# A perceiver layer: full-size fp32 scores, the 257th key on POOL, values of two batches together, both score pairs of a batch in a row

## The reference, cut to what matters

```python
# q: layernorm(x), 128 x 32 x 128;  k = v = ctx, 128 x 257 x 128;  16 heads of 8 channels
q = queries.reshape(B, L, H, 8); k = keys.reshape(B, 257, H, 8); v = k
scores = einsum('blhe,bshe->bhls', q, k)
A = softmax(scores / sqrt(8), axis=-1) * mask        # mask: 32 x 257, one for all batches
out = einsum('bhls,bshd->blhd', A, v)                # out is transposed by head and reshaped
x = x + out
```

## Time and profile before

| | us |
|---|---|
| median of 3 runs | 1129.01 (1126.96 to 1133.1) |
| profiled execution | 1124.33 |
| its span, first to last instruction | 1122.6 |
| busy: PE / DVE / ACT / POOL | 942.7 / 837.5 / 647.0 / 442.5 |
| mean granted TensorE clock | 0.947 of 2.4 GHz |

### The profile page before, as it was taken

One profiled execution on the slowest core, in us unless ns is written; L12 is line 12 of the kernel. 1 busy time (PEld: TensorE's weight loads), 2 busy tenths in 40 slices (PEclk: granted clock), 3 DMA queues, 4 the chain that ended last, 5 costly groups with the idle time before them and its releaser, 6 DMA issues. The chain is left out here.

```text
span 1122.6 us, 26586 instructions
## 1 busy us (share of the span) xinstructions
PE 942.7 (84%) x7948; PEld 749.0 (67%) x7948; DVE 837.5 (75%) x2150; ACT 647.0 (58%) x2006; POOL 442.5 (39%) x404
## 2 busy tenths in 40 slices
PE   4788888988888898888986788788799889898983
PEld 2455665656666565665655788788788778787873
DVE  4555777667677676767765988877669999999995
ACT  3434555555455555555552766666457767677774
POOL 2111212212122121212211544544357787787786
PEclk9878999899899989989997999988999999999997
DMA  1221111111011111111140000000000000000000
GB/s 56 60 60 34 41 33 33 31 33 39 25 42 31 33 31 33 43 31 33 31 133 1 1 0 0 0 0 0 1 1 6 7 7 9 5 9 5 9 5 15
DMA packets 32548, 27.15 MB, mean 24 GB/s; under 512 B 3532, under 2 KB 32264, under 8 KB 32520
## 3 DMA queue, kind: packets, MB, share of 16 engines
q1 hardware_dynamic: 32520, 26.80, 8.3%
HBM read 24.69 MB, written 2.10 MB: 24 GB/s over the span
## 5 line engine op out<-in xcount | busy, mean ns | idle before, releaser
L534 ACT ACTIVATE E<-SC,neg_max 128x257 f32<-128x257 f32 x512 | 238.3, 472 | 152.8 <-DVE neg_max L596 152.7
L604 DVE TENSOR_TENSOR Et<-ETP,mask_T 128x512 f32<-128x512 f32 x256 | 174.6, 682 | 116.6 <-PE ETP L409 116.6
L396 PE MATMUL SC<-Kt,Qbd 32*128 32x257 f32 x1024 | 181.1, 445 | 62.7 <-ACT E L534 36.3
L596 DVE TENSOR_REDUCE neg_max<-SC 128x2 f32<-128x514 f32 x256 | 174.6, 682 | 59.6 <-PE SC L396 59.6
L396 PEld LDWEIGHTS SC<-Kt,Qbd 32*128 32x128 f32 x1024 | 82.1, 193 | 114.5 <-ACT E L534 70.7
L1352 PE MATMUL PO<-W,hid 128*128 128x128 f32 x1024 | 138.2, 278 | 19.2 <-ACT hid L1393 19.1
L1352 PEld LDWEIGHTS PO<-W,hid 128*128 128x128 f32 x1024 | 131.4, 192 | 29.4 <-issue 21.6
L409 PE MATMUL ETP<-ident,E 128*128 128x128 f32 x1024 | 148.6, 291 | 0.8 <-ACT E L534 0.8
L1417 ACT ACTIVATE Y<-Z,zb,zs 128x128 f32<-128x128 f32 x256 | 111.0, 485 | 60.4 <-DVE zb L1572 60.4
L409 PEld LDWEIGHTS ETP<-ident,E 128*128 128x128 f32 x1024 | 119.3, 148 | 25.7 <-issue 23.6
L1341 PE MATMUL PH<-xT,W 128*128 128x256 f32 x512 | 135.1, 387 | 0.5 <-ACT xT L1385 0.5
(11 more groups left out here) (161 smaller groups left out, 1611.3 us busy)
## 6 DMA issues: line engine op xcount, KB each, us to landing
V<-in_ctx_dram SPq DMA_DIRECT2D x64, 256.0 KB, 2.7
xh<-in_x_dram SPq DMA_DIRECT2D x32, 64.0 KB, 2.1
last_rep<-in_ctx_dram SPq DMA_DIRECT2D x128, 2.0 KB
X<-in_x_dram SPq DMA_DIRECT2D x32, 64.0 KB
out_dram<-Xo SPq DMA_DIRECT2D x64, 32.0 KB, 1.5
W<-in_L_ffn_w_dram SPq DMA_DIRECT2D x1, 1024.0 KB
W<-in_L_ffn_w_dram SPq DMA_DIRECT2D x2, 512.0 KB
b2r<-in_L_ffn_b_dram SPq DMA_DIRECT2D x1, 512.0 KB
```

Source lines behind the costliest of these rows:

```text
L396: i = pe.matmul(SC[s % 2][:, u, 0:S], Qbd[r, h, jj, :], Kt[r, h, jj, 0:S], start=True, stop=True)
L534: i = act.activation(E[:, h, u0 + u, :], SC[s % 2][:, u, 0:S], ACT.Exp, bias=neg_max[:, s % 2, u:u + 1], accum_out=den[:, h, u0 + u:u0 + u ...
L596: dve.tensor_reduce(neg_max[:, s % 2, :], SC[s % 2][:, :, 0:S], AX.X, ALU.max, negate=True).then_inc(max_sb, 1)
L604: dve.tensor_tensor(Et[:, s % 4, :, :, :].rearrange("p u k c -> p (u k c)"), ETP[s % 2][:, :], mask_T[:, :, :, :].rearrange("p u k c -> p ...
```

## The change

The core of the diff, cut where lines only declare or rename:

```diff
@@ buffers
-            last_rep = sb1("last_rep", [HB * NQ, 2, D])
-            last_bd = sb1("last_bd", [HB * NQ, 2, HB, D])
+            last_row = sb1("last_row", [HB, 2, D])
+            last_all = sb1("last_all", [P, 2, HB, D])
-            Qbd = sb1("Qbd", [P, 2, HB, HQ * L])
+            Qbd = sb1("Qbd", [P, 2, HB, H, L])
-            Et = sb1("Et", [P, 4, 2, KT, HQ * L])
+            Et = sb1("Et", [P, HSTEPS, 2, KT, HQ * L])
@@ SP
             def load_last(sp, t, h):
-                for j in range(HB):
-                    sp.dma_start(last_rep[NQ * j:NQ * j + NQ, h, :], ...)
+                sp.dma_start(last_row[:, h, :], ctx[bass.ds(TB * t + HB * h, HB), S - 1, :]).then_inc(last_in[h], 16)
+            def load_all(sp, t, h):
+                sp.dma_start(last_all[:, h, :, :],
+                             ctx[bass.ds(TB * t + HB * h, HB), S - 1, :].unsqueeze(0).to_broadcast([P, HB, D])
+                             ).then_inc(all_in[h], 16)
                 def steps(t, fresh):
                     sp.wait_ge(xn_sb, 2 * t + 1)
                     load_x(sp, t + 1, 0)
+                    sp.wait_ge(qt_ps, 2 * t + 1)
+                    load_last(sp, t + 1, 0)
                     if not fresh:
                         sp.wait_ge(av_ps, TB * t)
                         load_ctx(sp, t, 3)
-                    sp.wait_ge(last_bd_set, 2 * t + 1)
-                    load_last(sp, t + 1, 0)
+                        sp.wait_ge(o_last, 2 * t)
+                        load_all(sp, t, 1)
                     if fresh:
                         for q in range(HQ // 2):
                             load_residual(q)
...
                     load_x(sp, t + 1, 1)
+                    sp.wait_ge(qt_ps, 2 * t + 2)
+                    load_last(sp, t + 1, 1)
                     sp.wait_ge(av_ps, TB * t + 4)
                     load_ctx(sp, t + 1, 1)
-                    sp.wait_ge(last_bd_set, 2 * t + 2)
-                    load_last(sp, t + 1, 1)
+                    sp.wait_ge(o_last, 2 * t + 1)
+                    load_all(sp, t + 1, 0)
                     if fresh:
                         for q in range(HQ // 2, HQ):
                             load_residual(q)
@@ POOL
+                def place_queries(t, h, j0=0, j1=HB, done=q_bd):
+                    pool.wait_ge(qt_sb, 2 * t + h + 1)
+                    pool.tensor_tensor(Qbd[:, h, j0:j1, :, :],
+                                       Qt[:, j0:j1, :].unsqueeze(2).to_broadcast([P, j1 - j0, H, L]),
+                                       head_scaled[:, :, :].unsqueeze(1).to_broadcast([P, j1 - j0, H, L]), ALU.mult).then_inc(done, 1)
+                def last_products(t, h):
+                    m = 2 * t + h
+                    pool.wait_ge(all_in[h], 16 * (t + 1))
+                    pool.tensor_tensor(last_x, last_all[:, h] by (batch group) x HQ x DK, block_of, ALU.mult).then_inc(v_last, 1)
+                    pool.tensor_tensor(last_y[:, :, :, :], last_x[:, :, 0:2, :], last_x[:, :, 2:4, :], ALU.add).then_inc(v_last, 1)
+                    pool.tensor_tensor(last_v[:, :, :], last_y[:, :, 0, :], last_y[:, :, 1, :], ALU.add).then_inc(v_last, 1)
+                    pool.wait_ge(p_last, m + 1)
+                    pool.tensor_tensor(last_o, last_v, last_p over DK, ALU.mult).then_inc(o_last, 1)
+                def add_last(t, h):
+                    pool.wait_ge(o_n, m + 1)
+                    pool.tensor_tensor(mine, mine, last_o[:, :, :], ALU.add).then_inc(o_both, 1)   # mine: O_n's half
                     for h in range(2):
                         place_queries(*((t, 1) if h == 0 else (t + 1, 0)))
+                        if h == 1 and not fresh:
+                            add_tile(t - 1)
                         power(t + 1, h)
-                        place_last(t, h)
-                        if h == 1 and not fresh:
-                            add_tile(t - 1)
+                            last_products(*((t, 0) if h == 1 else (t - 1, 1)))
+                            add_last(*((t, 0) if h == 1 else (t - 1, 1)))
...
-                place_queries(0, 0)
+                place_queries(0, 0, 0, 1, q_first)
+                place_queries(0, 0, 1, HB)
@@ TensorE
-                def turn_last(t, h):
-                    pe.transpose(LAST, E[:, h, :, S - 1], ident[:, :]).then_inc(lastt_ps, 1)
                 def scores(t, s, first=False):
...
-                        g = 2 * (s % 2) + u
-                        r = slice(32 * g, 32 * g + 32)
-                        i = pe.matmul(SC[s % 2][:, u, 0:S], Qbd[r, h, jj, :], Kt[r, h, jj, 0:S], start=True, stop=True)
+                        g = HQ * (2 * (s % 2) + u)
+                        i = pe.matmul(SC[s % 2][:, u, 0:S], Qbd[:, h, jj, g:g + HQ, :].rearrange("p q l -> p (q l)"),
+                                      Kt[:, h, jj, 0:S], start=True, stop=True)
-                def weigh_last(t, h):
-                    for j in range(HB):
-                        i = pe.matmul(AV[:, j, :], last_bd[:, h, j, :], last_Et[:, :], ...)
                 def lagging(t, s):
-                    if s % 2 == 1 and not (fresh and s < 5):
-                        tt, ss = back(t, s, 5)
-                        weigh_values(tt, ss // 2, first=fresh and s == 5)
+                    if s % 4 == 3 and not (fresh and s < HSTEPS - 1):
+                        tt, ss = back(t, s, 2 + 5)
+                        weigh_values(tt, ss // 2, first=fresh and s < HSTEPS)
+                        weigh_values(tt, ss // 2 + 1)
@@ DVE
-                def keep_last(t, h, final=False):
-                    dve.tensor_tensor(last_Et[:, :], LAST, mask_last[:, :], ALU.mult).then_inc(lastt_sb, 1)
+                def last_probs(t, h):
+                    dve.wait_ge(rden_set, m + 1)
+                    dve.wait_ge(o_last, m)
+                    dve.scalar_tensor_tensor(last_p[:, :], E[:, h, :, S - 1], mask_col[:, 0:1],
+                                             rden[:, :], ALU.mult, ALU.mult).then_inc(p_last, 1)
                 def keep_sums(t, h):
-                    dve.wait_ge(av_full, m + 1)
+                    dve.wait_ge(av_ps, HB * (m + 1))
                 def turn_tile(t):
-                    dve.wait_ge(o_n, 2 * t + 2)
+                    dve.wait_ge(o_both, 2 * t + 2)
...
-                        if s % HSTEPS == 1 and not (fresh and s < HSTEPS):
-                            keep_last(*((t, 0) if s > HSTEPS else (t - 1, 1)))
+                            if s % HSTEPS == 4:
+                                last_probs(tt, hh)
                             if s % HSTEPS == 5:
                                 own_outputs(tt, hh)
-                            if s == 6:
+                            if s == 7:
                                 turn_tile(tt)
```

More of the change, by code:

```diff
@@ L140, in perceiver_layer @@
             MISC = ps1("MISC", [P, 512])
-            QT_LAST = MISC[:, P:P + HB * NQ]
-            LAST = SC[1][0:HB * NQ, 1, 384:512]
+            QT_LAST = MISC[:, P:P + HB]
             ctx_in = [sem1(f"ctx_in{k}") for k in range(TB // 2)]
             last_in = [sem1(f"last_in{h}") for h in range(2)]
+            all_in = [sem1(f"all_in{h}") for h in range(2)]
             x_in = [sem1(f"x_in{h}") for h in range(2)]
@@ L268, in _ @@
                                    pattern=[[-DK, H]], channel_multiplier=1).then_inc(pool_set, 1)
-                pool.wait_ge(pool_set, 5)
+                pool.wait_ge(pool_set, 4)
                 pool.affine_select(out=head_of[:, :], in_=head_of[:, :], compare_op=ALU.is_ge, fill=0.0, base=DK - 1,
                                    pattern=[[DK, H]], channel_multiplier=-1).then_inc(pool_set, 1)
[L272 to L275, removed]
                 pool.iota(lag_i[:, :], pattern=[[-1, L]], base=0, channel_multiplier=1).then_inc(pool_set2, 1)
@@ L334, in _ @@
                 pool.memset(Vbd[:, :, :], 0.0).then_inc(pool_set2, 1)
+                pool.wait_ge(dve_set, 11)
                 run_tiles(steps, pool)
+                last_products(T - 1, 1)
+                add_last(T - 1, 1)
                 add_tile(T - 1)
@@ L384, in scores @@
                         pe.wait_ge(kl_sb, m + 1)
-                        pe.wait_ge(q_bd, m + 1)
+                        if first:
+                            pe.wait_ge(q_first, 1)
+                        else:
+                            pe.wait_ge(q_bd, m + 1)
+                    if isinstance(t, int) and t == 0 and s == 2:
+                        pe.wait_ge(q_bd, 1)
                     if not first:
                         pe.wait_ge(exp_sb, n - 1)
[L388 to L392, removed]
                     for u in range(2):
-                        g = 2 * (s % 2) + u
-                        r = slice(32 * g, 32 * g + 32)
-                        i = pe.matmul(SC[s % 2][:, u, 0:S], Qbd[r, h, jj, :], Kt[r, h, jj, 0:S], start=True, stop=True)
+                        g = HQ * (2 * (s % 2) + u)
```

(15 more changed lines are left out.)

115 lines of the change are left out of this document (56 added, 59 removed).

## The result

| | before | after |
|---|---|---|
| median of 4 runs, us | 1130.83 (1126.96 to 1133.1) | 1158.29 (1156.89 to 1159.2) |
| profiled execution / its span | 1124.33 / 1122.6 | 1159.2 / 1157.5 |
| end of cross attention in the trace | 603.8 | 636.9 |
| rest of the span | 518.8 | 520.6 |
| mean granted clock | 0.947 | 0.968 |

Ratio 1.0245, 95% interval 1.0211 to 1.028: slower by 27 us. The two profiled executions lie 34.9 apart in their spans, because the one of the kernel before was its fastest; 33.1 of that is in the first stage and 1.8 in the later ones.

What follows compares the result with a forecast made beforehand. A ring of waits through four engines bounds the first stage. Longer halves +39, first tiles −3 and clock −4 on the profiled 1124.33 give 1156.3; the median 2 to 4 higher, 1159 us, range 1146 to 1169.

Steps and rivals of the forecast that it cites:

- a ring of waits: First stage: odd scores, transpositions, mask product, odd maxima, exponentials, next odd scores pace a half; 17.32 us becomes 18.58.
- Ring and full-size scores: Odd score group in each pair of steps: next group 0.86 later instead of 0.63, net +0.23 us per pair.
- Forecast pairs: Times between odd score groups, steps 1 to 3, 3 to 5, 5 to 7, 7 to 1: 18.58 us in sum.
- The change of rows: TensorE, scores before transpositions: 0.20 of the 0.63 us is the change between 32 and 128 rows, no longer needed.
- The values behind which the keys wait: Pair from step 7 to 1: second batch of values adds 0.43 us ahead of the keys, bounds 0 and 0.57.
- keep_last and last_probs: DVE's order before the odd maxima: keep_last leaves pair 1, −0.20 us; last_probs enters pair 3, +0.10.
- POOL: Query blocks grow from 1.27 to 4.5 us and the last key's five operations take about 4; both covered, costing nothing.
- First tiles: Start of the kernel: residual loads reordered, first wait for x goes, second grows; together −3 us, from −8 to +4.
- Clock: Granted clock from 100 us on: two of four falls to half speed go, −4 us, between −9 and +20.
- the occupancy case: TensorE's summed work paces the half, which stays as is: 1117 us, chance 0.12; middle form 1125 to 1134, 0.07.
- The POOL case: POOL's last-key operations run late and get in DVE's way at turn_tile and normalise: about 1175 us, chance 0.13.
- The clock case: The clock falls more often, at the second stage's 0.91, costing 20 us more: 1180 us, chance 0.08.

Runs made afterwards that it cites:

- the run with single values: The changed kernel with the values of one batch at a time, five steps back, as before: 1147.9 us.
- the keys-first run: The changed kernel with the keys of step 0 (and of batch 4) turned ahead of the transpositions and values of the last pair: 1137.24 us.
- the fivefold run: The changed kernel with the first of POOL's five operations for the last key done five times instead of once: 1188.93 us.
- the maxima-first runs: The changed kernel and the kernel before, each with DVE's maxima of both steps ahead of the two mask products: 1124.30 us and 1102.96 us.

## Why the prediction was right

Forecast 1159, measured 1158.3. The mechanism, a ring of waits in which the full-size scores and the values ahead of the keys add time, is the one that the runs show. That the number is within 1 us is luck: several terms were off, and their errors cancelled.

- *Ring and full-size scores.* Forecast pairs 4.52, 4.48, 4.21, 5.37; measured 4.49, 4.54, 4.31 and 5.33 to 5.53 (the last without and with the end of the loop body). A half grew by 1.42 instead of 1.26. A group of full-size scores that starts after a pause occupies 0.97 (338.50 to 339.47), not the 0.86 of the experts' stream. That is so for steps 3, 5, 7 and 0; step 1, which follows step 0 at once, has 0.87 (334.01 to 334.88), and its pair came out as forecast. What stands behind the scores gave some of it back. The run with full-size scores alone has +1.67, the undoing of them (1148 to 1108) 40 us.
- *The change of rows.* The prediction took the whole 0.20 above two products side by side for the change between 32 and 128 rows. Full-size groups after a pause show 0.11 above their 0.86 with no change of rows before or behind them (328.48 to 329.45), so part of the 0.20 may be the price of a pause. No run separates the two.
- *The values behind which the keys wait.* Forecast 0.43 more ahead of the keys; the run with single values gives 0.41 a half back, the keys-first run 0.79.
- *keep_last and last_probs.* From the start of the latter to the maxima behind it are 0.15 (345.41 to 345.56), forecast 0.10. The forecast had −0.20 for the one and +0.10 for the other; the run that leaves only the last key on POOL has −0.27 a half in all.
- *POOL.* Query blocks 4.51, forecast 4.5. The five operations end at 349.71, 6.7 after the odd scores of step 5 (forecast "some 7"), turn_tile follows at 350.85 without waiting, 1.1 later, and the fivefold run showed where the cover ends.
- *First tiles.* The first wait went and the second grew by 5.0, to 8.6 (forecast 3.5, to 7.1). The sixth query block starts 3.97 later after the change. Four longer halves stand before it, which are 5.7, so the rest of the start gives −1.7 (forecast −3).
- *Clock.* Forecast −4, measured −8.6: all four falls went, not two.
- *Later stages and the median.* The later stages have 1.8 that nothing here explains (forecast 0). The forecast put the median 2.7 above the profiled execution; for the changed kernel it lies 0.9 below.

In sum, for the first stage: 26 halves between the sixth and the last query block × 1.42 = 36.9, − 8.6 for the clock, + 4.0 up to the sixth query block, + 0.8 at the end of the stage, 33.1. Against the forecast's terms: the longer halves cost 36.9 + 5.7 + 0.8 = 43.4 instead of 39, the first tiles −1.7 instead of −3, the clock −8.6 instead of −4, later stages +1.8 instead of 0, and the step to the median −0.9 instead of +2.7. The clock and the median paid for the rest.

Of the rivals, the occupancy case was wrong for both kernels, as the maxima-first runs show: there a half got shorter with the same work on TensorE. Its sums were wrong too. It put TensorE's work for a half at 14.8 before and 15.0 after. With most waits ordered away the changed kernel takes 15.7 and the kernel before 14.9, so even where occupancy paces the change costs about 20 us (1052 against 1033) and does not come out even. The POOL case did not occur: normalise takes 0.34 and 0.30 near 332 and 351. In the fivefold run it takes 0.83 in one half, from 347.05 to 347.88, beside a POOL operation that ends at 347.80, and costs nothing there. That is the exclusion which the Trainium skill (SBUF — State Buffer, who interferes with whom) describes. The clock case went the other way.

## What to carry to other kernels

Where no engine is full, find the ring of waits between the in-order queues and price an edit by what it adds there. Weighing two batches of values at once cost 10 us while TensorE waited, and gained 13 once it did not. Look first at the order inside one queue: two maxima ahead of two products, keys ahead of values and loads issued earlier gained some 100 us together, more than the layout change moved. And read the granted clock beside every time: one edit that the ring priced at −36 us came out at +43 with the clock at 0.75.

## What the runs showed of the hardware

- TensorE's granted clock did not follow the busy share in the profile: 347 us busy of 400 gave 0.75 with 32-row scores and paired values, 338 gave 0.99 with single values, 349 gave 1.00 with full-size scores. The first two kernels make the same products and differ only in when the values are weighed, and lie 94 us apart (1201.6 against 1107.6).
- Two full-size fp32 products of 257 columns (four records) occupy 0.97 after a pause and 0.86 to 0.87 behind others of their kind. Two on different 32-row strips occupy 0.63 to 0.64 where 128-row work follows, and four on four strips occupied 0.64 too where nothing between them waited.
- A DVE operation of 0.30 to 0.34 (normalise) took 0.83 (at 347.05 in the fivefold run) and 1.27 (at 10.30 before) where it started during a POOL operation. It ended at 347.88 and 11.57, the POOL operations at 347.80 and 11.49.
